# ScalarE instead of SP issues the 64 stores of the summed query weights in a cross-attention kernel

## What is computed

```python
q = (layernorm(x) @ Wq)          # 1024 x 4096: 32 heads of 128
k = ctx @ Wk ; v = ctx @ Wv      # 8 heads each
q, k = apply_rope(q), apply_rope(k)
logits = 30 * tanh(q @ k.T * 0.0884 / 30), masked
x = x + softmax(logits) @ v @ Wo
# then x = x + base(layernorm(x)) + routed rank-16 term
```

## Time and profile before

| | |
|---|---|
| Median of 3 runs | 2132.91 us (2132.7 to 2135.26) |
| Profiled execution, its own time | 2133.82 us |
| Its span in the profile | 2132.0 us |
| TensorE busy | 2121.2 us, 99% |
| VectorE, ScalarE, GpSimd busy | 78%, 41%, 16% |
| Chain that ended last | TensorE 95% |
| DMA, mean | 239 GB/s |

### The profile page before, as it was taken

How to read it: one execution, slowest core, us unless ns; L and a number is a source line. 1 busy time by engine, 2 the same in 40 slices (tenths; PEclk the granted TensorE clock), 3 DMA queues, 4 the chain that set the end, 5 groups by cost and what they waited for, 6 DMA issues and landing times.

```text
span 2132.0 us, 26530 instructions
## 1 busy us (share of the span) xinstructions
PE 2121.2 (99%) x9429; PEld 1721.4 (81%) x9429; DVE 1654.0 (78%) x2387; ACT 879.1 (41%) x1353; POOL 336.9 (16%) x438
## 2 busy tenths in 40 slices
PE   9999999999999999999999999999999999999999
PEld 7888887888888888877778777777787777888887
DVE  6969758999986666677878888998999898856533
ACT  3323343222241111147655556666666566423221
POOL 0000024666440000002111111111111110100000
PEclk9999999999999999999999999999999999999999
DMA  8778667777686665678665675578557854596761
GB/s 312 244 247 286 236 208 274 274 291 281 246 314 223 219 213 200 229 240 311 230 198 187 218 259 189 197 254 300 196 169 261 297 198 152 191 359 246 285 247 61
DMA packets 198820, 508.52 MB, mean 239 GB/s; under 512 B 20896, under 2 KB 46624, under 8 KB 196640
## 3 DMA queue, kind: packets, MB, share of 16 engines
q1 hardware_dynamic: 172448, 424.43, 57.1%
q0 software_dynamic: 26240, 82.38, 11.5%
HBM read 357.26 MB, written 149.16 MB: 238 GB/s over the span
## 4 chain that ended last, share of the span: by engine, by line
PE 95%; DMA 2%; DVE 1%; ACT 1%; issue 1%; SPq 0%; POOL 0%; ACTq 0%; DVEq 0%; POOLq 0%
PE pq L235 31%; PE pq L236 31%; PE pq L237 31%; PE pq L1300 1%; DMA RB<-rD 1%; DMA rD<-r 0%; PE pq L1949 0%; PE pq L1948 0%; DMA qraw<-gran 0%; DMA raw<-gran 0%; DMA kraw<-ctxT 0%; ACT Rh L1225 0%; DVE Rl L1230 0%; DVE Xq L744 0%; DVE pq L1544 0%
## 5 line engine op out<-in xcount | busy, mean ns | idle before, releaser
L235 PE MATMUL pq<-Ah,Rh 128*128 128x512 f32 x1024 | 399.0, 390 | 0.0
L237 PE MATMUL pq<-Ah,Rl 128*128 128x512 f32 x1024 | 398.5, 389 | 0.0
L236 PE MATMUL pq<-Al,Rh 128*128 128x512 f32 x1024 | 398.5, 389 | 0.0
L235 PE MATMUL pq<-Xq,qW 128*128 128x512 f32 x896 | 349.4, 390 | 2.2 <-DVE qp L1003 1.8
L236 PE MATMUL pq<-Xq,qW 128*128 128x512 f32 x896 | 349.3, 390 | 0.0
L237 PE MATMUL pq<-Xq,qW 128*128 128x512 f32 x896 | 349.1, 390 | 0.0
L1230 DVE TENSOR_TENSOR Rl<-raw,Rh 128x1024 fp32r<-128x1024 f32 x176 | 214.3, 1218 | 91.0 <-ACT Rh L1225 90.5
L1225 ACT ACTIVATE Rh<-raw 128x1024 fp32r<-128x1024 f32 x176 | 185.3, 1054 | 169.0 <-PE pq L237 130.9
L235 PEld LDWEIGHTS pq<-Ah,Rh 128*128 128x128 f32 x1024 | 192.2, 188 | 41.9 <-DVE Y L1529 0.8
L237 PEld LDWEIGHTS pq<-Ah,Rl 128*128 128x128 f32 x1024 | 192.2, 188 | 40.4
L236 PEld LDWEIGHTS pq<-Al,Rh 128*128 128x128 f32 x1024 | 192.2, 188 | 40.2
(11 more groups left out here) (243 smaller groups left out, 3934.3 us busy)
## 6 DMA issues: line engine op xcount, KB each, us to landing
raw<-gran SPq DMA_DIRECT2D x177, 512.0 KB, 4.3
QSD<-qW SPq DMA_DIRECT2D x64, 512.0 KB, 3.7
qD<-qt SPq DMA_DIRECT2D x128, 256.0 KB, 5.5
qW<-QSD SPq DMA_DIRECT2D x64, 512.0 KB, 3.5
qf<-qD SPq DMA_DIRECT2D x64, 512.0 KB, 6.0
RB<-rD POOLq DMA_DIRECT2D x128, 256.0 KB, 4.5
qraw<-gran SPq DMA_DIRECT2D x48, 512.0 KB, 4.8
kD<-kst SPq DMA_DIRECT2D x32, 512.0 KB, 5.7
```

What stands on the lines that cost most here:

```text
L235: e.matmul(dst, lh, rh, start=first, stop=False, skip_group_check=more)
L236: e.matmul(dst, lh, rl, start=False, stop=False, skip_group_check=more)
L237: return e.matmul(dst, ll, rh, start=False, stop=last, skip_group_check=more)
```

## The change

The loop that issues the stores is taken out of SP's step and put into ScalarE's step u, word for word, behind the high part for u + 5 and behind the Xq splits of the step. Its waits for the high and low part of w go with it. Nothing else changes; the number of instructions and DMAs is the same.

```diff
@@ act_q, step u (ScalarE) @@
                 if 0 <= u - 4 < NU and QP[u - 4][0] == 15:
                     x_high(t, 1, QP[u - 4][1])
+                todo = range(AHEAD) if u == 0 else range(u + AHEAD - 1, min(u + AHEAD, NU))
+                for w in todo:
+                    n, i = QP[w]
+                    if SRC[i][0] == "S" and n < 16:
+                        z = (w + 1) % NQW
+                        t.wait_ge("q_hi", w)
+                        t.wait_ge("q_lo", w)
+                        e.dma_start(QSD[n, SRC[i][1]], f(qW[z][:, :, :])).then_inc(*t.tick(f"d_qk{z}", w, 16))
                 act_att_early(t, u)
@@ sp_q, step u (SP) @@
                     e.dma_start(f(qW[z][:, :, :]), QSD[n - 16, SRC[i][1]]).then_inc(*t.tick(f"d_qw{z}", w, 16))
-                todo = range(AHEAD) if u == 0 else range(u + AHEAD - 1, min(u + AHEAD, NU))
-                for w in todo:
-                    n, i = QP[w]
-                    if SRC[i][0] == "S" and n < 16:
-                        z = (w + 1) % NQW
-                        t.wait_ge("q_hi", w)
-                        t.wait_ge("q_lo", w)
-                        e.dma_start(QSD[n, SRC[i][1]], f(qW[z][:, :, :])).then_inc(*t.tick(f"d_qk{z}", w, 16))
                 if u < NU and QP[u][1] == 2 and QP[u][0] < 30:
                     n = QP[u][0] + 2
```

## The result

The forecast was 2129.3 us. The changed kernel takes 2138.27 us, median of 22 runs (2135.13 to 2141.36). The kernel before, run beside it, takes 2132.80 us (22 runs, 2130.57 to 2137.39). The ratio is 1.0022, with a 95% interval of 1.0016 to 1.0028: slower, and outside the range given. The profiled execution of the changed kernel took 2138.89 us, with a span of 2137.1.

The account below looks back on a forecast made before the run. TensorE was taken as the bound, with one 3.65 us stop in the query projection. That term, the others being 0, off the median of 2132.91 gave 2129.3 us, 0.17% less; range 2128.2 to 2133.2.

Parts of the forecast that it names:

- What bounds the kernel, and what the stop costs: TensorE busy 2121.2 of 2132.0 us; its halt before product 10 costs 1.99 us late start plus 1.67 us lower clock.
- the stop: TensorE's halt ahead of product 10 in the query projection, waiting for VectorE's addition at L1003; 3.65 us with the clock loss.
- a term of 3.65: Predicted gain of 3.65 us from removing TensorE's whole halt ahead of product 10, late start and clock loss together.
- What the change removes: SP loads qraw for n = 2 at about 320.1 instead of 334.4; VectorE's 2.94 us wait at L774 goes: -3.65 us.
- What it adds on ScalarE: 64 store issues of 0.33 to 0.98 us lie in ScalarE's idle time: term 0, up to +3.65 if TensorE stops once.
- ring: ScalarE waits for VectorE's split while VectorE's additions wait for ScalarE's copy at L984; each halt of TensorE about 3.65 us.
- the bound from SP's rows (0.98): Upper price of one store issue on ScalarE, 0.98 us, taken from SP's issues: 0.32 least, 0.33 median.
- What moves in the DMA queues: First three stores no longer queue behind the Xq loads; Xq[6] still ready for product 6: term 0, bounds 0 and +3.65.
- put to the worst: All three first stores (1.57 MB, 3.7 us) go ahead of the last Xq load, which then lands at 331.9 instead of 328.2.
- The list of what would prove the forecast wrong: TensorE waiting at product 3 (late copy) or 6 (late Xq[6]), or over 2 us idle in later rows for L1003 or splits.
- the first: Rival: no change, 2132.9 us, as L1003 is late from another cause, such as a stretched split or slightly late Xq[6]; chance 0.18.
- the third: Rival: slower, as ScalarE and VectorE hold each other in a ring; three halts of TensorE make 2140.2 us; chance 0.07.

Follow-up runs that it names:

- load_first: Kernel before with SP's load of the query weights moved ahead of SP's own stores, nothing on ScalarE: 2130.59 us (0.9985); repeated 2131.87 us (0.9992).
- halves: Changed kernel with each of the three first stores issued as two DMAs with rows of 2 KB instead of 4 KB: 2136.06 us (1.0012).
- first3_act: Kernel before with only the stores of w = 1, 2, 3 issued by ScalarE, the 61 others left with SP: 2140.15 us (1.003).
- late_load: Changed kernel with SP's load of qraw for n = 2 held back until the split of w = 8, as before the change: 2140.34 us (1.003).
- mid_act: load_first with the six stores of w = 6 to 15 issued by ScalarE, the other 58 by SP: 2134.40 us (1.0007).

## Why the prediction was wrong

**What bounds the kernel, and what the stop costs.** Right. With the load ahead and nothing else changed (load_first) the stop goes and the time falls by 3.3 us (2133.89 to 2130.59) and by 2.0 us in the repeat, against a term of 3.65. The query projection, from its first product to the first matmul of the next stage, takes 610.0 us instead of 613.7 and 614.1.

**What the change removes.** Right, step by step: the load at 319.93 (forecast 320.1), no wait at L774, product 10 on time.

**What it adds on ScalarE.** Right for this kernel: 0.33 to 0.42 us for each of the three, the copy not late, no ring. (In the second profile one issue of the 64 took 1.43 us.) halves shows that the bound from SP's rows (0.98) was too low: 1.5 us for each of three in a row.

**What moves in the DMA queues.** Here the prediction failed. It set the term to 0 by asking one question only, whether the last part of Xq[6] is ready for product 6, and found 1.4 us to spare. Two things were wrong.

First, the sizes. It took the last load to land by 331.9 "put to the worst", 15.2 us behind the first product. ScalarE met it at 332.90, which is 16.8 us behind (15.5 to 16.4 in the other three profiles), up to 1.6 us beyond that bound. The early loads of qraw are not shown to be the reason: first3_act and late_load, which issue them later, have 15.8 and 15.9. Nor was there time to spare at product 6, by an estimate from these rows: the last low part of Xq[6] was done at 337.0 (333.45 + 3.56), and without the stop at product 5 product 6 would have read it at 316.14 + 18.4 = 334.5. The stop ahead of product 5 hid that.

Second, the place. It counted the last load and not the one ahead of it. The second half of Xq[5] moved from 324.70 to 329.65, and VectorE's work on it stands ahead of L1015, which product 5 waits for. In the kernel before, that addition ran with time to spare (VectorE, then the first matmul of product 5):

```profile
325.37 1.29 DVE L744 TENSOR_TENSOR Xq<-Xq 128x512 fp32r<-128x512 f32 x2 [1.11 <-ACT Xq L734]
...
327.80 0.69 DVE L1007 TENSOR_TENSOR qp<-pq,qp 128x512 f32<-128x512 f32 x1 [0.54 <-PE pq L237]
```

```profile
330.32 0.39 PE L235 MATMUL pq<-Xq,qW 128*128 128x512 f32 x1
```

L1007 waited 0.54 us for TensorE and ended at 328.49, 1.83 us ahead of product 5: 2.37 us to spare. Counted from the first product (316.72 before, 316.14 after), ScalarE had the second half of Xq[5] at 7.98 before and at 13.51 after, 5.53 us later. The difference, 3.16 us, is the late start of product 5. In the other three profiles of the kernel after the same sum gives 1.71, 3.44 and 2.55 us, and product 5 starts 1.72, 3.45 and 2.55 us late. The time to spare could be read in the trace of before. The list of what would prove the forecast wrong named products 3 and 6, not 5. Of the rivals, the first came nearest with "a slightly late Xq[6]", but it had the wrong load, and no change as its result; the third, the only slower one, put the cost in a ring of ScalarE and VectorE that no trace shows.

**Later rows.** The prediction has no term for GpSimd's loads of Bx. It looked at who waits for SP's queue ("TensorE waits for none of them") and not at what else shares the DMA engines with the new one.

**The account.** Mean loss by stops in the query projection, four profiles after: product 5 with (5.9 + 1.8 + 5.1 + 4.2)/4 = 4.3 us, product 17 with (0 + 4.2 + 2.3 + 2.3)/4 = 2.2. Before, product 10 with (3.65 + 4.1)/2 = 3.9. Difference 2.6 us. The stage itself took 616.0, 616.3, 617.5 and 616.9 us after (mean 616.7), 613.7 and 614.1 before (613.9): 2.8 us. These six executions differ by 3.5 us in their spans (mean 2136.2 and 2132.75), and the 0.7 us that is left lies mostly in the first 60 us of the attention, which took 61.0 to 64.1 us after and 60.5 and 62.0 before. That part is 60.2 to 64.1 us long in all kernels, copies included, so this is not shown to be the change's. The medians differ by more, by 5.5 us in the comparison shown and by 4.4 us against the kernel before in a later comparison (2133.89). The two profiled executions of the kernel before (2133.82 and 2135.3 us) lie above its median of 2132.80, the four after (mean 2138.06) near theirs; no faster execution of the kernel before was profiled, and where those are faster stays open.

**Two rules on the queues.** The Trainium skill (DMA: Bandwidth & Descriptors, Queues, rings and completion order) says that an engine goes in turn through the queues that have work, packet by packet. The traces agree that both queues are served in turn (above) and that the loads are late by it; what one turn holds they leave open, since strict turns of one row each would give 1.0 in packets where 0.71 and 0.77 were seen. The prediction quoted it, saw that stores and loads would share, and still took the end at which nothing is late. The other rule (same page, Issuing engines are not separate DMA queues), by which another issuing engine saves issue time only, would have kept the time at 2132.9. The runs speak against that reading: the choice of the engine chose a queue, and with it whose transfers are late, 4.7 us for the Xq loads (8.3 to 13.0) and about 4 us for those of Bx (4.2 or 4.3 in load_first, 8.3 in mid_act).

## What to carry to other kernels

A DMA moved to another engine can move to another queue (here from q1 to q10), where it no longer stands behind the loads that were issued ahead of it; for each such load, not only the last, go through the work that stands in order behind it, and ask what is late if it lands several microseconds later. If a queue blocks on a wait, first try to turn the order round inside that queue: here one block moved down in SP's loop gave the gain, and moving the stores to ScalarE lost it twice.

## What was not expected of the hardware

- The bytes that a queue got went with the size of what it was given: 1.39 times those of SP's queue with stores of 512 KB in rows of 4 KB and 0.72 times with 256 KB in rows of 2 KB, at nearly the same ratio of packets.
- An addition of VectorE (L782) took 2.26 us with GpSimd busy beside it and 4.74 us when GpSimd had two splits and an addition without a pause; L774 took 5.87 us beside three splits and an addition. Each ended 0.56 us behind the unbroken run, so a pause of 0.23 us of GpSimd was worth 2.5 us. Additions of the same size elsewhere took 0.68.
- Over the profiles of all kernels the granted clock fell to 0.50 behind 13 stops with 1.8 to 3.3 us of idle time and stayed at 1.00 behind 11 others with 1.6 to 2.6. Where it fell it cost 1.4 to 1.7 us, and once 2.8; where it did not, 0.1. So the price of one and the same stop differs by about 1.7 us between executions.
- Three DMA issues on ScalarE in a row, with three more just ahead of them, took 1.5 us each instead of 0.33.
